# Query projection of the second layer as seven block products for groups 3 to 6, on one Trainium2 core

## The reference

```python
q = (hidden_states @ Wq.T).reshape(bsz, q_len, H, HD).transpose(0, 2, 1, 3)
q = _rmsnorm(q, q_norm_w)
k = _rmsnorm(k, k_norm_w)
scores = jnp.einsum('bhqd,bhkd->bhqk', q, k) * scale
probs = jax.nn.softmax(scores.astype(jnp.float32), axis=-1).astype(q.dtype)
out = jnp.einsum('bhqk,bhkd->bhqd', probs, v)
return out.reshape(bsz, q_len, H * HD) @ Wo.T
```

## Time and profile before

| | |
|---|---|
| median of 3 runs | 1179.61 us (1178.96 to 1181.38) |
| the profiled execution's own time | 1179.01 us |
| its span, first to last instruction | 1177.1 us |
| mean granted clock of TensorE | 0.999 |
| busy share of PE, DVE, POOL, ACT | 99%, 75%, 45%, 36% |

### The profile page before, as it was taken

How to read it: one execution, slowest core, us unless ns; L and a number is a source line. 1 busy time by engine, 2 the same in 40 slices (tenths; PEclk the granted TensorE clock), 3 DMA queues, 4 the chain that set the end, 5 groups by cost and what they waited for, 6 DMA issues and landing times.

```text
span 1177.1 us, 17132 instructions
## 1 busy us (share of the span) xinstructions
PE 1169.5 (99%) x6272; PEld 946.7 (80%) x6272; DVE 880.9 (75%) x1538; ACT 424.0 (36%) x748; POOL 532.9 (45%) x371
## 2 busy tenths in 40 slices
PE   9999999999999999999999999999999999999998
PEld 8888888888788888777788888777777777777776
DVE  4656646898888888889984335798888887888695
ACT  5145152322322222231552123535453443435542
POOL 5522533766667676677463112305242433425410
PEclk9999999999999999999999999999999999999999
DMA  7944735812211221211210003121221221121101
GB/s 286 285 137 159 211 111 162 287 55 81 81 66 59 89 80 45 80 45 45 99 64 36 1 1 107 55 94 57 91 80 45 80 80 54 71 89 39 43 1 72
DMA packets 57315, 106.54 MB, mean 91 GB/s; under 512 B 3633, under 2 KB 36529, under 8 KB 51889
## 3 DMA queue, kind: packets, MB, share of 16 engines
q1 hardware_dynamic: 56736, 104.82, 26.0%
q0 software_dynamic: 384, 1.05, 0.2%
q10 hardware_dynamic: 144, 0.00, 0.0%
HBM read 78.59 MB, written 27.26 MB: 90 GB/s over the span
## 4 chain that ended last, share of the span: by engine, by line
PE 96%; DVE 2%; issue 0%; ACT 0%; DVEq 0%; POOL 0%; POOLq 0%
PE ps_q L226 14%; PE ps_b L226 14%; PE ps_b L228 14%; PE ps_b L227 14%; PE ps_q L227 13%; PE ps_q L228 13%; PE ps_s L978 5%; PE ps_b L1005 4%; PE ps_s L278 1%; PE ps_q L953 1%; PE ps_q L2152 1%; PE ps_b L479 1%; PE ps_s L1847 1%; PE ps_q L529 0%; PE ps_b L529 0%
## 5 line engine op out<-in xcount | busy, mean ns | idle before, releaser
L226 PE MATMUL ps_q<-hT_hi,wq_hi 128*128 128x512 f32 x512 | 203.2, 397 | 0.0
L227 PE MATMUL ps_q<-hT_lo,wq_hi 128*128 128x512 f32 x512 | 199.6, 390 | 0.0
L228 PE MATMUL ps_q<-hT_hi,wq_lo 128*128 128x512 f32 x512 | 199.2, 389 | 0.0
L226 PE MATMUL ps_b<-wo_hi,o_hi 128*128 128x512 f32 x440 | 171.6, 390 | 0.0
L227 PE MATMUL ps_b<-wo_lo,o_hi 128*128 128x512 f32 x440 | 171.2, 389 | 0.0
L228 PE MATMUL ps_b<-wo_hi,o_lo 128*128 128x512 f32 x440 | 171.2, 389 | 0.0
L743 POOL TENSOR_TENSOR wq_lo<-wq_raw,wq_hi 128x512 fp32r<-128x512 f32 x64 | 90.2, 1413 | 112.8 <-ACT wq_hi L737 112.8
L1317 POOL TENSOR_TENSOR qT<-q_t 128x512 f32<-128x512 f32 x64 | 89.8, 1405 | 66.3 <-DVE q_t L1430 60.8
L226 PEld LDWEIGHTS ps_q<-hT_hi,wq_hi 128*128 128x128 f32 x512 | 96.1, 188 | 24.3 <-issue 1.5
L228 PEld LDWEIGHTS ps_q<-hT_hi,wq_lo 128*128 128x128 f32 x512 | 96.1, 188 | 20.3
L227 PEld LDWEIGHTS ps_q<-hT_lo,wq_hi 128*128 128x128 f32 x512 | 96.2, 188 | 18.7
(11 more groups left out here) (301 smaller groups left out, 2498.0 us busy)
## 6 DMA issues: line engine op xcount, KB each, us to landing
wq_raw<-in_wq SPq DMA_DIRECT2D x16, 1024.0 KB, 4.8
wo_raw<-in_wo SPq DMA_DIRECT2D x16, 1024.0 KB, 4.8
kT<-kT_spill SPq DMA_DIRECT2D x32, 256.0 KB, 4.3
v_hi<-v_hi_spill SPq DMA_DIRECT2D x16, 512.0 KB, 3.7
v_lo<-v_lo_spill SPq DMA_DIRECT2D x16, 512.0 KB, 4.7
v_hi_spill<-vs_hi SPq DMA_DIRECT2D x12, 512.0 KB, 5.4
v_lo_spill<-vs_lo SPq DMA_DIRECT2D x12, 512.0 KB, 6.7
kw_raw<-in_wk SPq DMA_DIRECT2D x4, 1024.0 KB, 9.2
```

Source lines behind the costliest of these rows:

```text
L226: nc.tensor.matmul(dst, l_hi, r_hi, start=first, stop=False)
L227: nc.tensor.matmul(dst, l_hi, r_lo, start=False, stop=False)
L228: return nc.tensor.matmul(dst, l_lo, r_hi, start=False, stop=last)
```

## The change

In the second layer, groups 3 to 6 (W0 = 3, eight steps), the projection of the four heads of a group for 512 tokens is taken as a 2x2 block product: the 512 input features in two halves, the four heads in two pairs (`WD` = 256 columns), the 512 tokens in two quarters (`QT` = 256). In place of eight block products there are seven, of sums of blocks (Winograd's form). The parts:

- Weights: four sums s1 to s4 of quarter blocks per group on GpSimd (128x512 elements each), seven high parts on ScalarE (`woven_high`), seven low parts on GpSimd (`woven_low`), in place of four high and four low parts of 128x512.
- Tokens: four mixed blocks t1 to t4, once for the layer, from the normed input's high and low parts: ten 128x1024 sums and four low parts on GpSimd, four high parts on ScalarE, in steps (1, 0) to (2, 1).
- TensorE: 7 x 12 matmuls of 256 columns per step (`project_woven`) in place of 4 x 12 of 512.
- Combining the products: per step four joins on VectorE (PSUM plus SBUF), one addition on GpSimd, and copies and squares on ScalarE. The eight copies of the norm sums go to ScalarE in these steps (`sums_by_quadrant`), the fold becomes two 64x1024 operations in place of four 64x512, and three of the four output additions stand behind `p_lo`.
- The query and key norm weights are multiplied into the keys at their staging, not into the queries. The loop of the second layer becomes `Fori(3, 6)` with steps 2 and 6 written out. Buffers move; the transposed probabilities use `s_sb` in most steps.

```diff
+        WOVEN_PARTS = ("a11", "s2", "s3", "a12", "s1", "a22", "s4")
+        def woven_sums(pool, gt):
+            pool.wait_ge(*c("wq_in", 16 * (gt + 1)))
+            nc.gpsimd.tensor_tensor(s1_f, s1_f, a22, ALU.add).then_inc(c["s_f"], 1)
...
+            nc.gpsimd.tensor_tensor(s2_f[:, :, :], s1_f, a11, ALU.subtract).then_inc(c["s_f"], 1)
...
+            nc.gpsimd.tensor_tensor(s3_f[:, :, :], a22, s2_f[:, :, :], ALU.subtract).then_inc(c["s_f"], 1)
...
         def att_wq_split(sp, lay, n):
+            if lay and n > W0:
+                sp.wait_ge(*att[lay]("woven_hi", 7 * (n - W0)))
+                sp.wait_ge(*att[lay]("woven_lo", 7 * (n - W0)))
+                return
...
+            def project_woven(g, h):
+                    for q in range(2):
+                        for k in range(2):
+                            nc.tensor.matmul(dst, l_hi[:, k, col], r_hi[:, k, :], start=first and (q, k) == (0, 0), stop=False, skip_group_check=True)
+                            nc.tensor.matmul(dst, l_hi[:, k, col], r_lo[:, k, :], start=False, stop=False, skip_group_check=True)
+                            last = nc.tensor.matmul(dst, l_lo[:, k, col], r_hi[:, k, :], start=False, stop=closes, skip_group_check=True)
...
+                pe.wait_ge(*c("ssq_t", u))
+                product(ps_q[0], "a11", tokens(0, 0), True).then_inc(c["product"], 1)
+                product(ps_q[1], "s2", mixed(t2_hi, t2_lo), True, True).then_inc(c["product"], 1)
+                pe.wait_ge(*c("s_turned", u))
+                product(ps_h[0], "s3", mixed(t3_hi, t3_lo), True).then_inc(c["product"], 1)
+                pe.wait_ge(*c("copied", 2 * n + 1))
+                product(ps_q[0], "a12", tokens(1, 0), False, True).then_inc(c["q_done"], 1)
+                product(ps_h[1], "s1", mixed(t1_hi, t1_lo), True).then_inc(c["q_done"], 1)
+                pe.wait_ge(*c("joined", 4 * n + 2))
+                product(ps_h[0], "a22", mixed(t4_hi, t4_lo), False, True).then_inc(c["q_done"], 1)
+                pe.wait_ge(*c("copied", 2 * n + 2))
+                product(ps_h[1], "s4", tokens(1, 1), False, True).then_inc(c["q_done"], 1)
...
+            def woven_step(g, h, next_wq):
+                if h == 0:
+                    for name in WOVEN_PARTS[4:]:
+                        woven_low(pool, g, name)
+                    for j in range(J):
+                        wo_low(g - 1, j)
+                elif building:
+                    woven_low(pool, g + 1, "a11")
+                att_shift(pool, lay, u - 1)
+                pool.wait_ge(*c("copied", 2 * n + 2))
+                pool.wait_ge(*c("joined", 4 * n + 2))
+                nc.gpsimd.tensor_tensor(qT[:, h, 2:4, late], qT[:, h, 2:4, late], q_sq[:, 2:4, late], ALU.add).then_inc(c["c22_made"], 1)
+                if h and building:
+                    woven_last_sum(pool, g + 1)
...
+                att_normalise(pool, lay, u - 1)
+                if h == 0 and not (isinstance(g, int) and g == G - 2):
+                    woven_sums(pool, g + 1)
+                elif building:
+                    for name in WOVEN_PARTS[1:4]:
+                        woven_low(pool, g + 1, name)
```

More of the change, by code:

```diff
@@ L19 @@
 JS = J * S
+QT = HALF // 2
+WD = 2 * D
+W0 = 3
 SC = PAIRS * JS
@@ new lines, in woven_high @@
+        def woven_high(act, gt, name):
+            c = att[1]
+            first = isinstance(gt, int) and gt == W0
+            last_use = 2 * gt - 1 - 2 * W0
+            act.wait_ge(*c("wq_in", 16 * (gt + 1)))
+            if name in ("a11", "a12") and first:
+                act.wait_ge(*c("q_done", 8 * gt - 2))
+            elif name in ("s1", "a22") and first:
+                act.wait_ge(*c("q_done", 8 * gt))
+            elif name in ("a11", "s2", "s3") and not first:
+                act.wait_ge(*c("product", 3 * last_use + ("a11", "s2", "s3").index(name) + 1))
+            elif name != "s4" and not first:
+                act.wait_ge(*c("q_done", 8 * gt - 3 + ("a12", "s1", "a22").index(name)))
+            if name[0] == "s":
+                act.wait_ge(*c("s_f", 4 * (gt - W0) + int(name[1])))
+            f, hi, lo = woven_parts(name)
+            nc.scalar.activation(hi, f, ACT.Copy).then_inc(c["woven_hi"], 1)
@@ L1067, in step @@
                         values(up, h, g - 1)
+                if woven(lay, g):
+                    project_woven(g, h)
+                    for t in range(PAIRS):
+                        project_out(up, h, g - 1, t)
+                    return
                 at_first = lay and isinstance(g, int) and (g, h) == (0, 0)
@@ new lines, in step @@
+                if lay and isinstance(g, int) and (g, h) == (1, 1):
+                    att_wq_low(pool, lay, 2, 0)
+                    att_shift(pool, lay, us)
+                    pool.wait_ge(*c("p_exp", us + 1))
+                    mixed_first(t3_f, t3_t, (1, 1), (0, 1))
+                    att_normalise(pool, lay, us)
+                    for j in range(1, J):
+                        att_wq_low(pool, lay, 2, j)
+                    pool.wait_ge(*c("p_lo", us + 1))
+                    mixed_joined(t3_f, t3_t, 6)
+                    mixed_next(t2_f, (1, 1), t1_f, 8, 3)
+                    return
@@ new lines, in step @@
+                if lay and isinstance(g, int) and (g, h) == (2, 0):
+                    for j in range(J):
+                        wo_low(1, j)
+                    att_shift(pool, lay, us)
+                    pool.wait_ge(*c("p_exp", us + 1))
+                    mixed_next(t4_f, (1, 0), t2_f, 10, 8)
+                    att_normalise(pool, lay, us)
+                    woven_sums(pool, W0)
+                    pool.wait_ge(*c("p_lo", us + 1))
+                    mixed_low(t1_lo, t1_hi, t1_f, 1)
+                    return
@@ L1403, in att_pool @@
                 pool.wait_ge(*c("mask_in", 16))
-            att_steps(pool, step)
+            att_steps(pool, lay, step)
             if lay:
@@ L1434, in turn_scores @@
                 dve.wait_ge(*c("scored", u + 1))
+                if lay and not (isinstance(u, int) and (u < 4 or u == 2 * G - 1)):
+                    dve.wait_ge(*c("p_lo", u))
                 nc.vector.transpose(s_sb[:, :], ps_s[:, :]).then_inc(c["s_turned"], 1)
@@ L1530, in add_output, with woven_step, joined @@
                                                ALU.mult, ALU.add).then_inc(c["y_added"], 1)
+            def woven_step(g, h):
+                u, us, up = 2 * g + h, 2 * g + h - 1, 2 * g + h - 2
+                n = u - 2 * W0
+                heads = lambda bank: bank.rearrange("p (j t) -> p j t", j=2)
+                early, late = slice(0, QT), slice(QT, HALF)
+                part_b, part_d = qT[:, h, 0:2, late], qT[:, h, 2:4, late]
+                def joined(out, bank, part):
+                    return nc.vector.tensor_tensor(out, heads(bank), part, ALU.add)
+                turn_sums(us, 1 - h, True)
+                turn_scores(us, 1 - h)
+                scale_scores(us)
+                dve.wait_ge(*c("copied", 2 * n + 1))
+                dve.wait_ge(*c("product", 3 * n + 2))
+                joined(part_b, ps_q[1], part_b).then_inc(c["joined"], 1)
+                att_mask(dve, lay, us, 1 - h)
+                dve.wait_ge(*c("joined", 4 * n + 1))
+                dve.wait_ge(*c("product", 3 * n + 3))
+                joined(part_d, ps_h[0], part_b).then_inc(c["joined"], 1)
+                maxima(us)
+                out_low(up, 0)
+                out_low(up, 1)
+                dve.wait_ge(*c("q_done", 4 * u + 3))
+                joined(qT[:, h, 2:4, early], ps_h[0], part_b).then_inc(c["joined"], 1)
+                out_low(up, 2)
+                dve.wait_ge(*c("q_done", 4 * u + 4))
+                joined(part_b, ps_h[1], part_b).then_inc(c["joined"], 1)
+                out_low(up, 3)
+                sums(us)
+                add_output(up, h, 0)
+                fold_woven(u, 0)
+                turn_probs(us)
+                fold_woven(u, 1)
+                att_probs_low(dve, lay, us)
+                for t in range(1, PAIRS):
+                    add_output(up, h, t)
             def step(g, h, do_project, do_score, do_finish, next_wq):
```

284 lines of the change are left out of this document (246 added, 38 removed).

## The result

The changed kernel takes 1199.45 us (median of 5 runs, 1198.63 to 1200.04) where the kernel before takes 1179.45 in the same session: a ratio of 1.0167, 95% interval 1.0153 to 1.0181. The prediction was 1203 (1184 to 1213), slower with 0.82. So the sign, the size and the mechanism came out.

A forecast was written before the change was run, and what follows sets the result against it. TensorE, busy 99% of the span, was taken to bound the kernel, with VectorE's exclusions setting the pace after the change: 1179.0 + 6 (rewritten steps, matmul saving included) + 18 (mixing steps) = 1203 us, range 1184 to 1213.

The forecast's parts named there:

- Term 1: TensorE in the eight rewritten steps: 84 matmuls at 0.119 us replace 48 at 0.2267, saving 0.88 us a step.
- The bound with exposed loads: Rewritten steps: 0.19 us per matmul if weight loads do not overlap, 5.1 us lost a step; as a rival, chance 0.05.
- Term 2: Rewritten steps: VectorE's 23.3 us queue plus 3.7 us of GpSimd meetings makes 27.0 us; net 6 us lost, matmul saving included.
- The forecast of who is late: Rewritten steps: VectorE's last output additions, awaited by the next value products, and the splits before the output products are late.
- Term 3: Steps (1,1), (2,0), (2,1): GpSimd mixing overtakes VectorE's small copies and later operations, losing 6, 8 and 4 us, together 18.
- Step (7,0): Step after the last rewritten one: nothing was put on it, and the last rewritten step gains about 0.5 us.
- Free edits: Norm weights in the keys' existing copy, fewer semaphore increments, ScalarE's added copies and later query-weight transfers cost nothing.
- The clock: Whole kernel: nothing put for a lower granted clock, though TensorE's waits of several us might lower it.
- Only the opening steps pay: Rival: rewritten steps stay TensorE's, gaining 7 us, while the three mixing steps cost 16: 1188 us; chance 0.17.

The follow-up runs named there:

- e4: Changed kernel with three GpSimd weight sums and six of seven weight low parts of groups 4 to 6 cut to 4 columns: 1193.83 us, ratio 1.0126.
- e11: e9 with two GpSimd waits changed, for the joining operation in step (1,1) and the fourth weight sum in (2,1): 1175.68 us, ratio 0.9970.
- e8: Kernel before with the 512-column query-projection matmuls of groups 2 to 6, second layer, each written as two of 256 columns: 1185.57 us, ratio 1.0058.
- e3: Changed kernel with its 14 GpSimd mixing operations cut to 4 columns and the mixed-token products fed plain token blocks: 1180.27 us, ratio 1.0011.
- e1: Changed kernel with the eight small copies of steps (1,1), (2,0) and (2,1) made by ScalarE: 1190.51 us, ratio 1.0095.
- e6: Changed kernel with GpSimd reordered in rewritten steps: weight sums, last low parts and plain splits wait for the probabilities' low part: 1196.69 us, ratio 1.0148.
- e9: e7 with GpSimd's backlog reduced, an output split before the small maxima, and two mixing operations on VectorE in step (1,1): 1178.62 us, ratio 0.9993.
- e7: Changed kernel with the edits of e1 and e6, mixing begun earlier, and TensorE waiting for each mixed block only at its product: 1184.95 us, ratio 1.0049.

## Why the prediction was right, point by point

**Term 1, the matmuls: right.** Predicted 0.119 apart and 0.88 us saved a step; measured 0.12, and 26.07 - 25.13 = 0.94 where nothing else is late (e4, e11). The bound with exposed loads did not occur. e8 shows the surplus per matmul, 13 ns, by itself.

**Term 2, VectorE's step: the mechanism right, the net wrong even in sign.** Predicted 27.0 us a step and 6 us lost net; measured 26.36 and 25.70, 26.03 in the mean, about the 26.07 of before: the meetings eat up the saving of term 1 and no more. The 0.9 lost over the eight steps come from (3,0); with the mixing cut the eight gain 1.6 (e3). Both parts of the sum were too large. Meetings: counted 3.7, measured 3.3 a step. In the second step of the pair these are fold 1.25, fold 1.08 and low part 0.97; in the first, fold 1.25, low part 0.97, scaling 0.54 (1.77 for 1.23) and mask 0.49 (1.72 for 1.23). The queue without them: put at 23.3, measured 26.03 - 3.3 = 22.7, in part because the eight operations that read PSUM start 0.61 apart when they follow each other, not 0.66 (0.4 of the 0.6). The forecast of who is late was right: TensorE waits for the additions to `x_sb`, up to 1.9 us at a time. That removing the meetings makes the steps TensorE's own was shown by e4. Step (3,0) at 28.6 stands out; e3 shows that 2.6 of it belong to the mixing before it. It is TensorE's own 25.2, 1.9 of waiting for the additions to `x_sb`, and 1.5 of lower clock (e4).

**Term 3, the three mixing steps: right in its sum, incomplete in its reason.** Predicted 6, 8 and 4, measured 5.75, 8.09 and 3.85. The copies lost 4.3, 8.5 and 3.5 against 4.4, 8.8 and 3.5 counted, and the assumption that SBUF copies take part holds. What the sum did not say is that the folds are a second way by which the cost reaches TensorE (6.2 us of its waits in front of the scores), and that the copies shielded what stands behind them. e1 took the copies away, and scaling, mask and small maxima were overtaken in their place; only half came back.

**Step (7,0): missed.** The prediction let the last rewritten step gain and put nothing on the next. The group after still needs three plain splits; they now stand behind the normalisation of step (6,1) and meet VectorE's fold and low part, and the three additions behind them are late for the value products of (7,0). e6, which moves these splits, takes off 1.07 of the 1.61; with one of them behind the first fold instead (e9) it is gone, though e9 changed other things in these steps too, so the last 0.54 is not pinned on that edit.

**Free edits: right as far as seen.** The scaling in the keys' copy and the later weight transfers show no wait of TensorE for a transfer in any of the changed steps.

**The clock: put at nothing**, and it took 1.5 us in step (3,0) (e4, and below).

So 1199.45 against 1203 is a sum of errors that partly cancel: 5 too much for the rewritten steps, 0.3 too much for the mixing, 1.6 too little for (7,0). Divided as e3 divides it, with all that the mixing brings put down to the mixing, it is 18 forecast against 19.2, 6 lost against 1.6 gained in the rewritten steps, and nothing against 1.6 in (7,0) and 0.95 in (2,1). In the rewritten steps the rival *Only the opening steps pay* was nearer (7 gained). That the forecast's total came closer owes something to luck.

## What to carry to other kernels

Before moving elementwise work to GpSimd, list VectorE's operations with two SBUF inputs and its SBUF copies, and the stretches in which it works from PSUM, reduces, transposes or waits; only the latter are free. Here each queued GpSimd operation got ahead of one exclusive VectorE operation, even one of 32x16, so a train of small ones is the worst neighbour. Waits put ahead of GpSimd operations, on the event that ends VectorE's exclusive stretch, made most of the difference between 1199.45 and 1175.68 together with the moved copies, more than the 7.5 us of matmuls saved. They also push work on, and it can meet something else there (e6, e7). Take away a cost at one place and read the trace again before counting it as gained: the collision may have moved to the next instruction.
